# A vision and text block with a mixture of experts on one core: the two experts of a token from VectorE's MAX and MAX_INDEX

## What is computed

```python
logits = jnp.einsum('gsd,de->gse', xg, w_router)
probs = jax.nn.softmax(logits, axis=-1)
gate, idx = jax.lax.top_k(probs, TOP_K)              # TOP_K = 2 of E = 8
idx_kf = jnp.swapaxes(idx, 1, 2).reshape(G, TOP_K * S)
mask = jax.nn.one_hot(idx_kf, E, dtype=jnp.int32)
prio = jnp.cumsum(mask, axis=1) * mask - 1           # place of a token in its expert's queue
...
dispatch = jax.nn.one_hot(prio_se, C, dtype=x.dtype) # C = 60 places
expert_in = jnp.einsum('gsec,gsd->egcd', dispatch, xg)
```

## Time and profile before

| | |
|---|---|
| median of 3 runs | 370.7 us |
| the runs | 370.23, 370.7, 374.36 us |
| the profiled execution | 373.86 us |
| its span, first to last instruction | 372.1 us |
| mean granted TensorE clock | 0.957 |
| busy: PE, DVE, ACT, POOL | 339.2, 207.2, 97.9, 40.7 us |

### The profile page before, as it was taken

One profiled execution on the slowest core, in us unless ns is written; L12 is line 12 of the kernel. 1 busy time (PEld: TensorE's weight loads), 2 busy tenths in 40 slices (PEclk: granted clock), 3 DMA queues, 4 the chain that ended last, 5 costly groups with the idle time before them and its releaser, 6 DMA issues. The chain is left out here.

```text
span 372.1 us, 8648 instructions
## 1 busy us (share of the span) xinstructions
PE 339.2 (91%) x3654; PEld 248.3 (67%) x3654; DVE 207.2 (56%) x643; ACT 97.9 (26%) x188; POOL 40.7 (11%) x87
## 2 busy tenths in 40 slices
PE   4899859999899889999999999999999998979685
PEld 3776446788567436785966858668867676758485
DVE  3917446699998983234333343333446367686644
ACT  1223613665543341011010110101021233312230
POOL 8503220210101102000000000000111110110100
PEclk9999969999999899999999999999999999995858
DMA  7959940000000004999099140000000000000004
GB/s 268 341 126 268 271 106 2 4 4 4 2 4 2 3 0 96 187 188 245 16 222 202 45 127 0 3 0 0 2 2 0 2 3 0 3 2 0 0 3 127
DMA packets 27044, 26.75 MB, mean 72 GB/s; under 512 B 4379, under 2 KB 23197, under 8 KB 27005
## 3 DMA queue, kind: packets, MB, share of 16 engines
q1 hardware_dynamic: 26108, 25.60, 28.8%
q10 hardware_dynamic: 896, 0.59, 0.7%
HBM read 24.91 MB, written 1.28 MB: 70 GB/s over the span
## 5 line engine op out<-in xcount | busy, mean ns | idle before, releaser
L701 PEld LDWEIGHTS banks<-sb_wo_sl,sb_attn_hidT_attn 128*128 128x128 f32 x384 | 62.2, 190 | 5.6 <-issue 4.9
L701 PE MATMUL banks<-sb_wo_sl,sb_attn_hidT_attn 128*128 128x192 f32 x384 | 64.5, 328 | 0.0
L1703 DVE COPY sb_w_tok_e_out<-banks 60x384 f32<-60x384 f32 x32 | 17.8, 555 | 49.8 <-PE banks L701 49.3
L683 PE MATMUL banks<-sb_tok_xeT,sb_wi_sl 128*128 128x480 f32 x96 | 40.1, 567 | 1.1 <-ACT sb_tok_xeT L1202 1.1
L1217 ACT ACTIVATE sb_attn_hidT_attn<-banks 128x480 f32<-128x480 f32 x24 | 13.7, 571 | 102.8 <-PE banks L688 102.8
L1693 DVE TENSOR_SCALAR sb_attn_hidT_attn<-banks 128x480 f32<-128x480 f32 x24 | 15.8, 658 | 27.8 <-PE banks L688 25.9
L683 PEld LDWEIGHTS banks<-sb_tok_xeT,sb_wi_sl 128*128 128x128 f32 x96 | 18.0, 190 | 18.9 <-issue 17.0
L472 PE MATMUL banks<-sb_tok_xeT 128*32 128x193 f32 (+1 forms) x512 | 24.8, 328 | 0.8 <-DMA sb_tok_xeT<-in_xhalo 0.8
L472 PEld LDWEIGHTS banks<-sb_tok_xeT 128*32 128x32 f32 (+1 forms) x512 | 17.1, 109 | 6.7 <-issue 4.1
L688 PE MATMUL banks<-sb_tok_xeT,sb_wi_sl 64*128 64x480 f32 x96 | 21.5, 580 | 0.0
L594 PE MATMUL banks<-sb_w_v,sb_xrT 97*32 97x96 f32 x512 | 14.9, 269 | 4.3 <-issue 4.3
(11 more groups left out here) (238 smaller groups left out, 543.8 us busy)
## 6 DMA issues: line engine op xcount, KB each, us to landing
sb_wo_sl<-in_wo SPq DMA_DIRECT2D x8, 576.0 KB, 7.3
sb_tok_xeT<-in_xin SPq DMA_DIRECT2D x8, 448.0 KB, 5.6
sb_onehot_combT<-route_rows SPq DMA_DIRECT2D x6, 512.0 KB, 9.4
sb_wi_sl<-in_wi SPq DMA_DIRECT2D x8, 288.0 KB, 4.7
sb_wi_sl<-in_wi SPq DMA_DIRECT2D x24, 96.0 KB, 4.8
sb_xn<-route_rows SPq DMA_DIRECT2D x4, 512.0 KB, 11.0
sb_w_tok_e_out<-in_wtok SPq DMA_DIRECT2D x2, 960.0 KB, 7.0
sb_attn_hidT_attn<-route_rows SPq DMA_DIRECT2D x2, 512.0 KB, 12.7
```

Source lines behind the costliest of these rows:

```text
L683: nc.tensor.matmul(PS[:, HID_BANKS[f], 0:SLOTS], wi_sl[:, q, f * 128:(f + 1) * 128], xeT[:, 0, e].rearrange("k g c -> k (g c)"), start=Tru ...
L701: mm = nc.tensor.matmul(PS[:, 4 + j // 2, j % 2 * D:(j % 2 + 1) * D], hidT[:, e % 2, f, j * 128:(j + 1) * 128], wo_sl[:, q, f], start=(f = ...
L1703: ve.tensor_copy(e_out[64 * (e % 2):64 * (e % 2) + CAP, hf * 4 + z:hf * 4 + z + 3:2, e // 2], PS[64 * z:64 * z + CAP, 4 + hf, 0:2 * D].rea ...
```

## The change

The chain's maximum becomes VectorE's MAX, which writes the eight largest values of a row in falling order; with 8 experts it sorts the tile's logits. MAX_INDEX then writes the positions of these eight values. Both take one row per partition, so there is one instruction per tile (three per group). The first two positions are compared with 0 to 7 in one instruction that writes both experts' rows. A new helper `step` counts an instruction on the semaphore without a wait, and `settle` waits for all that were counted; the three MAX go without a wait between them, as do the subtraction from the maximum and the three MAX_INDEX. The subtraction moves from `choose_first` to `choose`. `r_top` is replaced by `r_best` and `r_at`; the constant `rev` is still loaded.

```diff
--- before.py
+++ after.py
@@ -6,6 +6,7 @@
 ALU = mybir.AluOpType
 ACT = mybir.ActivationFunctionType
 F32 = mybir.dt.float32
+U32 = mybir.dt.uint32
 AX_X = mybir.AxisListType.X
 AX_XY = mybir.AxisListType.XY
 
@@ -174,7 +175,8 @@
         r_exp = sb("r_exp", [128, TILES, E])
         r_sums = sb("r_sums", [128, 2, TILES])
         r_sum = sb("r_first_sum", [128, J, E])
-        r_top = sb("r_top", [128, 3, NB])
+        r_best = sb("r_best", [128, NB, 8])
+        r_at = sb("r_at", [128, NB, 8], U32)
         r_e = sb("r_e", [128, 2, NB, E])
         slot_of = sb("slot_of", [128, TILES, E])
         gate_of = sb("gate_of", [128, TILES, E])
@@ -1545,6 +1547,13 @@
                 ins.then_inc(sem("r_step"), 1)
                 ve.wait_ge(sem("r_step"), steps[0])
 
+            def step(ins):
+                steps[0] += 1
+                ins.then_inc(sem("r_step"), 1)
+
+            def settle():
+                ve.wait_ge(sem("r_step"), steps[0])
+
             def wide(x, n=NB):
                 return x.unsqueeze(2).to_broadcast([128, n, E])
 
@@ -1582,8 +1591,9 @@
             def choose_first(j):
                 lg = logits[:, J]
                 ve.wait_ge(sem("r_logit"), j + 1)
-                then(ve.tensor_reduce(r_top[:, 0], lg, AX_X, ALU.max))
-                then(ve.tensor_tensor(r_exp[:, NB * j:NB * j + NB], lg, wide(r_top[:, 0]), ALU.subtract))
+                for blk in range(NB):
+                    step(ve.max(r_best[:, blk], lg[:, blk]))
+                settle()
 
             def scale_routes(j):
                 own = r_exp[:, NB * j:NB * j + NB]
@@ -1592,19 +1602,15 @@
 
             def choose(j):
                 lg = logits[:, J]
-                rev = const("rev").unsqueeze(1).to_broadcast([128, NB, E])
-
-                def pick(src, best, dst):
-                    then(ve.tensor_tensor(r_e[:, 0], src, wide(best), ALU.is_equal))
-                    then(ve.tensor_tensor(r_e[:, 0], r_e[:, 0], rev, ALU.mult))
-                    then(ve.tensor_reduce(r_top[:, 1], r_e[:, 0], AX_X, ALU.max))
-                    then(ve.tensor_tensor(dst, r_e[:, 0], wide(r_top[:, 1]), ALU.is_equal))
-
-                pick(lg, r_top[:, 0], first_of(j))
-                then(ve.scalar_tensor_tensor(r_e[:, 1], first_of(j), -3e38, lg, ALU.mult, ALU.add))
+                step(ve.tensor_tensor(r_exp[:, NB * j:NB * j + NB], lg, wide(r_best[:, :, 0]), ALU.subtract))
+                for blk in range(NB):
+                    step(ve.max_index(r_at[:, blk], r_best[:, blk], lg[:, blk]))
+                settle()
+                both = [128, NB, 2, E]
+                then(ve.tensor_tensor(choice[:, j, 0:5:2].rearrange("t b (k e) -> t b k e", k=2),
+                                      const("iota")[:, 0:E].unsqueeze(1).unsqueeze(1).to_broadcast(both),
+                                      r_at[:, :, 0:2].unsqueeze(3).to_broadcast(both), ALU.is_equal))
                 ve.tensor_reduce(r_sum[:, j], first_of(j).rearrange("t b e -> t e b"), AX_X, ALU.add).then_inc(sem("r_choice"), 1)
-                then(ve.tensor_reduce(r_top[:, 2], r_e[:, 1], AX_X, ALU.max))
-                pick(r_e[:, 1], r_top[:, 2], second_of(j))
                 ve.tensor_tensor(choice[:, j, 1:4:2], choice[:, j, 0:3:2], choice[:, j, 2:5:2], ALU.add).then_inc(sem("r_choice"), 1)
 
             def place(j):
```

## The result

| | before | after |
|---|---|---|
| median of 20 runs each | 372.03 us | 368.97 us |
| lowest to highest | 369.93 to 376.56 | 364.17 to 373.48 |
| the profiled execution, its span | 373.86, 372.1 | 368.35, 366.2 |
| mean granted clock in it | 0.957 | 0.972 |

The medians differ by 3.06 us. The ratio is 0.9894, with a 95% interval of 0.9863 to 0.9925, so 2.8 to 5.1 us. The ratios here leave out runs that lie over 1.5% above the fastest of their kernel, which can be 1 of 12 runs of the one kernel and 10 of 17 of the other, so I give the medians over all runs beside them.

The account below looks back on a forecast made before the run. TensorE bounds the kernel, but waits for VectorE's four routing chains. Each chain 1.1 us shorter, 4.4 in all, cut off to 2.5 at TensorE: 370.7 - 2.5 = 368.2 us, range 365.6 to 370.4.

Parts of the forecast that it names:

- The chain's price: VectorE's expert-choice chain, once per group: falls from 2.79 to 1.68 us, 1.1 us shorter each.
- the 0.10 per unwaited step: In the chain, an instruction without a wait starts 0.10 us behind its neighbour; with a wait, 0.215.
- The slow end: Chain's upper bound: nine MAX and MAX_INDEX steps at 0.29 us, chain 3.28; as rival "Slower" 372.7 us, chance 0.07.
- Nothing overlaps: Rival: each new chain instruction takes a full 0.215 us step, 0.76 us saved in all, 369.9 us; chance 0.12.
- The cut-offs: Routing stage: each chain's 1.1 us gain is limited by whatever then comes last; 2.5 us of 4.4 reaches TensorE.
- Chain 3's step: Last group: the 0.66 and 0.40 us of TensorE idle go, adding 1.06 to 1.45 for 2.5 us.
- Chain 0: First group: VectorE then waits for scores(2), ending at 85.74 us, so the gain is 0.7 us, not 1.1.
- The 0.66 in front of L642: TensorE's idle 0.66 us at 125.78, put down to ScalarE by the profile, counted as VectorE's.
- even a much faster MAX_INDEX: In the chains: a still lower price for the index search gives no more than 2.5 us at TensorE.
- The clock: Third dispatch's half-rate fall may go, 1.5 us more; left out of the median; as rival 366.7 us, chance 0.32.
- everything behind moving as a whole: From the experts' start (L683, 137.86 us) TensorE's own list bounds, so what is gained before is kept.
- Lost behind: Rival: L683 starts earlier but late stages' half-rate stretches give the gain back, 370.7 us; chance 0.09.

Follow-up runs that it names:

- waits_back: The changed kernel with a wait behind every MAX and MAX_INDEX and behind the subtraction; 374.2 us (1 run).
- after_again: The changed kernel executed and traced a second time, nothing altered; 372.5 us (1 run).
- add_first: The changed kernel with add_attention(2) ahead of score_max(3, 2) in VectorE's list instead of behind it; 370.47 us (12 runs).
- last_only: The new chain for group 3 alone, the old chain for groups 0 to 2; 374.57 us (1 run).
- last_old: The new chain for groups 0 to 2, the old chain for group 3; 372.56 us (1 run).
- values_only: The changed kernel without MAX_INDEX, comparing the logits with the two largest values; 369.76 us (6 runs), ratio 0.9942 to the kernel before.

## Why the prediction was right

**The size.** The forecast was 2.5 us; measured are 3.06 between the medians, and 2.8 to 5.1 by the ratio. The time after, 368.97 us, lies in the range. The median before of 20 runs is 372.03, 1.3 above the 370.7 that I had, so of the 0.8 us between the forecast, 368.2, and 368.97 the base gives 1.3 and the larger gain takes back 0.5.

**The chain's price.** Forecast 1.68 us, measured 1.42: 1.37 shorter, not 1.1. By the rows of chain 0: three MAX with their wait 0.35 (forecast 0.415), the subtraction 0.10 (0.10), three MAX_INDEX with their wait 0.53 (0.715), the comparison 0.25 (0.24), the reduction 0.09 (0.10), the addition 0.10 (0.11). The term that was mis-sized is the 0.10 per unwaited step: between MAX8, load and search it is 0.07. MAX_INDEX has two steps, as I took it. The slow end (RECIPROCAL's 0.29 each) was far off. *Nothing overlaps* is refuted by the starts 0.07 us apart, and `waits_back` shows that even then the chain would be 2.23 and not 2.60, because a load starts its search 0.08 behind it without a wait between. The Trainium skill's "The DRAIN you can't avoid" ("VectorE: DVE Perf Modes") has the next instruction wait until the pipe is empty, but adds that one which is not held starts earlier. Taken by the first sentence alone, as the rival took it, the trace disagrees for these instructions, 0.07 us between starts against 0.15 to 0.16 of length; with the addition it agrees. That section of the Trainium skill also has a semaphore between instructions cost nothing extra; here the waits cost 0.81 us in one chain.

**What of it reaches TensorE.** The cut-offs are as described. From the start of D, TensorE is earlier at these points (the forecast in front of L642 of group 3 is 1.45 and the 0.66 of idle time):

| at | forecast | after | after_again |
|---|---|---|---|
| first wait for `h` (95.85 before) | 0.7 | 0.96 | 0.87 |
| second wait for `h` (111.87) | 1.1 | 1.49 | 1.12 |
| `choice` of group 2 (117.71) | 1.45 | 1.90 | 1.53 |
| `choice` of group 3 (125.78) | 2.1 | 2.64 | 2.26 |
| third dispatch (127.22) | 2.5 | 3.07 | 2.70 |

VectorE waits in front of `score_max(2, 0)` (0.32) and `score_max(3, 0)` (0.74) with L608 as releaser, and the 0.71 at L243 stays, all as written. Chain 3's step was counted as TensorE's idle time, 0.66 and 0.40; its real limit, `mark_slots(2)` behind `dispatch_tails(0)`, was not in it. That the two come out alike, 1.06 and 1.2, is luck. Chain 0 gave more than 0.7: `scores(2)` had 0.22 and 0.31 of score idle in these two traces and not the 0.59 of before, so it ended earlier. This term I had not seen. With as much of it as before, chain 0 gives what was forecast: in `add_first`, whose lists up to there are those of the changed kernel, it is 0.58, and TensorE is 0.61 earlier at the first wait for `h`. I took the end of `scores(2)` at 85.74 as fixed, and it moves by up to 0.6 us from execution to execution; this moves the gain at the third dispatch between 2.7 and 3.1. The 0.66 in front of L642, which I counted as VectorE's against the profile's releaser, was VectorE's, by `last_only` and `last_old`.

**No more from a shorter chain.** The forecast said that even a much faster MAX_INDEX gives no more than 2.5. It holds with another size: `values_only` gives 46.08 - 43.33 = 2.75, as much as after_again. At the other end `waits_back` saves 0.56 us per chain and gives 46.08 - 44.28 = 1.8, where the forecast's steps come to about 2.0 (twice 0.56, the idle 0.34 and 0.56 again).

**The clock.** I left its 1.5 us out of the median, since half-rate stretches differ between equal programs. Two of three traces of before have the fall and one hasn't, so it is neither absent nor always there. But the price was wrong too. E is 56.71 and 56.79 with the fall and 55.94 without: 0.8 us, because the wait for `mark_slots(3)` in `dispatch_tails`, whose length I had not looked at, lies under the longer dispatch (`dispatch_tails` lasts 3.50 without the fall and 2.75 and 2.65 with it). The idle time in front doesn't decide alone: eight traces have the 0.4 us and two of them the fall. None of the six without it has the fall. Whether the change removes the fall or the count is luck stays open.

**What comes after L683.** The forecast counted on everything behind moving as a whole. For 197 us behind the experts' start it does, to 0.02 us. Up to the experts the traces without the fall differ by 2.8 to 3.1 in E, the two with it by 3.5 to 4.0, and the medians over whole executions by 3.06. *Lost behind* is not borne out. The 2.3 us by which the two profiled executions differ in the last stage are not put down to the change: the clock's line of the changed kernel's second trace ends in 5868 and not in 6969. From the 2.3 us wait at L241 to the end, the five traces with the shortest E (52.80 to 53.58) take 31.6 to 35.5 us and the nine others 32.3 to 37.9. Whether that is more than chance is not shown.

## What to carry to other kernels

Shortening a wait-bound chain on a side engine pays until the other engine's own work comes last; find that point for each repetition from the starts and ends in the trace, and stop there, because beyond it only the side engine's waits grow. In a chain of dependent short instructions, take those that don't need each other's results out of the waits: here that was a third of the gain or more. Check a releaser that the profile names against the code, and look within groups of matmuls for waits that count as "issue": the one in `dispatch_tails` was missed here for that reason.

## What the runs showed of the hardware that I had not expected

- In the trace of after, MAX8 over 8 values lasts 0.15 us (0.150 to 0.170), MATCH_VALUE_LOAD 0.07, FIND_INDEX8 0.16. Without waits they start 0.07 apart; in `waits_back`, with a wait, a MAX8 starts about 0.22 behind the last and a pair of load and search 0.27.
- Matmuls of `scores`, 32 rows by 96 columns, have a stretch of idle time put down to "issue" that differs from execution to execution of one program: 0 to 0.61 us in one group and 0 to 0.71 in the other over the fourteen traces. It goes with a transfer of 16 KB on the queue that the traces call q8, instruction; each trace has 29 of them, 65 bytes for each of TensorE's 7,308 matmuls and weight loads. In group 2 the idle time is there in the eight traces in which such a transfer ends 0.00 to 0.41 us behind the first matmul of the scores, and absent in the six in which it ends 0.08 to 0.28 ahead of it. In group 3 it is there in nine, with ends 0.15 to 0.55 behind, and absent in five, with ends from 0.01 ahead to 0.15 behind. In all seventeen places TensorE goes on 1.2 to 1.5 us after the transfer has ended. That TensorE waits for its own instructions there is my reading of this; no run tried it.
- The clock's fall in the third dispatch comes and goes with identical idle time ahead, and costs 0.8 us at the experts' start, not the 1.5 of the dispatch itself.
